# Two-tile cluster transposes, a block-diagonal coarse product, and other engines for the last two pairs of a fused language-model layer

## What is computed

```python
fine_emb = fine_embed_w[location_ids]                                   # 64 columns
cluster_logits = loc_to_cluster_w.T[location_ids] + loc_to_cluster_b    # 64 clusters
cluster_dist = softmax(cluster_logits, axis=-1)
coarse_emb = einsum('bsc,ch->bsh', cluster_dist, coarse_embed_w)        # 64 columns
h = concatenate([fine_emb, coarse_emb], axis=-1)
...
# per expert e, with gate weight g of each token for each expert
y += g * (silu(x @ w_gate[e].T) * (x @ w_up[e].T)) @ w_down[e].T
```

## Time and profile before

| | |
|---|---|
| time, median of 3 runs | 710.78 us (710.51 to 711.16) |
| profiled execution | 710.27 us |
| its span, first to last instruction | 708.1 us |
| TensorE's granted clock over it | 1.000 |
| busy: PE, DVE, ACT, POOL | 693.4 (98%), 472.1 (67%), 389.5 (55%), 465.6 (66%) us |
| mean DMA rate over the span | 113 GB/s |

### The profile page before, as it was taken

The page is one execution under the profiler, slowest core; times in us unless marked ns, Lnnn a source line. Parts: engine busy times, 40 slices in busy tenths (PEclk is TensorE's granted clock), DMA queues, the critical chain, the costliest instruction groups (busy, mean ns, idle before and its releaser), DMA issues.

```text
span 708.1 us, 10029 instructions
## 1 busy us (share of the span) xinstructions
PE 693.4 (98%) x3130; PEld 521.2 (74%) x3130; DVE 472.1 (67%) x976; ACT 389.5 (55%) x719; POOL 465.6 (66%) x359
## 2 busy tenths in 40 slices
PE   8789999999999999999999999999999999999998
PEld 7766776777777777777777777777777777777775
DVE  5687666775686765966578756876669555774443
ACT  3555466548456566557565484565665555534333
POOL 5036776766768567777577666685676666676664
PEclk9999999999999999999999999999999999999999
DMA  5504332333233333253233332343333433344431
GB/s 201 235 0 126 124 104 101 116 115 106 89 121 124 105 120 104 84 148 96 100 110 116 112 114 90 119 124 100 120 104 91 132 99 106 112 122 120 137 120 59
DMA packets 48869, 80.17 MB, mean 113 GB/s; under 512 B 9520, under 2 KB 13744, under 8 KB 48816
## 3 DMA queue, kind: packets, MB, share of 16 engines
q1 hardware_dynamic: 47792, 77.44, 34.6%
q0 software_dynamic: 1024, 2.10, 1.3%
HBM read 76.35 MB, written 3.15 MB: 112 GB/s over the span
## 4 chain that ended last, share of the span: by engine, by line
PE 89%; DVE 4%; issue 2%; ACT 1%; POOL 1%; DVEq 0%; ACTq 0%; POOLq 0%
PE bank_y L487 16%; PE bank_g L504 8%; PE bank_u L504 8%; PE bank_u L506 8%; PE bank_u L505 8%; PE bank_g L506 8%; PE bank_g L505 8%; PE bank_y L484 4%; PE bank_y L482 4%; PE bank_y L481 4%; PE bank_f L406 1%; PE bank_f L428 1%; PE bank_f L465 1%; PE bank_f L422 1%; PE bank_f L439 1%
## 5 line engine op out<-in xcount | busy, mean ns | idle before, releaser
L1145 POOL TENSOR_TENSOR hid<-hid,gate_rows 128x512 f32<-128x512 f32 x256 | 370.9, 1460 | 195.2 <-DVE hid L961 193.6
L961 DVE TENSOR_TENSOR hid<-hid,bank_u 128x512 f32<-128x512 f32 x258 | 175.3, 683 | 172.7 <-PE bank_u L506 93.4
L680 ACT ACTIVATE hid<-bank_g 128x512 f32<-128x512 f32 x264 | 156.8, 597 | 209.6 <-PE bank_g L506 201.4
L487 PE MATMUL bank_y<-hid,w_down 128*128 128x512 f32 x280 | 142.7, 592 | 0.1
L504 PE MATMUL bank_g<-x_hi,gate_hi 128*128 128x512 f32 x264 | 141.4, 536 | 0.8 <-ACT hid L680 0.8
L974 DVE TENSOR_TENSOR hid_lo<-hid,hid_hi 128x512 fp32r<-128x512 f32 x124 | 115.1, 928 | 1.0 <-ACT hid_hi L686 0.5
L504 PE MATMUL bank_u<-x_hi,up_hi 128*128 128x512 f32 x264 | 104.9, 397 | 0.3 <-DVE hid L961 0.3
L506 PE MATMUL bank_u<-x_lo,up_hi 128*128 128x512 f32 x264 | 104.8, 397 | 0.0
L505 PE MATMUL bank_u<-x_hi,up_lo 128*128 128x512 f32 x264 | 104.1, 395 | 0.0
L506 PE MATMUL bank_g<-x_lo,gate_hi 128*128 128x512 f32 x264 | 103.9, 394 | 0.0
L505 PE MATMUL bank_g<-x_hi,gate_lo 128*128 128x512 f32 x264 | 103.8, 393 | 0.0
(11 more groups left out here) (223 smaller groups left out, 845.8 us busy)
## 6 DMA issues: line engine op xcount, KB each, us to landing
gate_rows<-gates_dram SPq DMA_DIRECT2D x512, 128.0 KB, 2.9
w_down<-down_t_dram SPq DMA_DIRECT2D x3, 704.0 KB, 14.5
out_dram<-later SPq DMA_DIRECT2D x7, 256.0 KB, 3.1
hid<-gate_t_dram SPq DMA_DIRECT2D x2, 704.0 KB, 6.6
gates_dram<-gates_t SPq DMA_DIRECT2D x8, 128.0 KB, 2.3
gate_rows<-up_t_dram SPq DMA_DIRECT2D x1, 704.0 KB, 5.9
later<-up_t_dram SPq DMA_DIRECT2D x1, 704.0 KB, 10.2
raw<-gate_t_dram SPq DMA_DIRECT2D x1, 704.0 KB, 11.2
```

What stands on the lines that cost most here:

```text
L487: pe.matmul(y, w_down[:, p, :], hid[:, slot(par, p), :], start=(p == 0), stop=(p == PAIRS - 1)).then_inc(sem("down_done"), 1)
L680: act.activation(hid[:, slot(par, p), :], bank_g[(p + par) % 2][:, :], ACT.Silu).then_inc(sem("silu"), 1)
L961: dve.tensor_tensor(hid[:, s, :], hid[:, s, :], bank_u[(p + par) % 2][:, :], ALU.mult)\
L1145: pool.tensor_tensor(hid[:, s, :], hid[:, s, :], gate_rows[:, row, :], ALU.mult)\
```

## The change

Three things change.

1. The transposes take two tiles at once: 128 tokens x (2 x 64) clusters become a 128x128 block, so there are two where there were four, and the result fills 128 partitions x 256 columns. ACT's copy has that shape too.
2. The coarse weight is laid out block-diagonally in a 128x128 tile, zeroed by a DVE memset and filled by two DMAs, which SP issues after a wait for the memset. Two matmuls with 128 rows and 128 columns take the place of four with 64 rows and 64 columns; the output lies as it did.
3. In the last sequence pair 31 is no longer split, and pair 32's gate weights are multiplied on by DVE in place of POOL. DVE does it at the end of its list, after its own product of pair 32, and TensorE's last `down` waits for that.

```diff
-        coarse_sb = sb("coarse_sb", [CLUSTERS, HALF])
+        coarse_sb = sb("coarse_sb", [P, 2 * HALF])
...
-        lge_t = z[0:CLUSTERS, :, :].rearrange("p t d -> p (t d)")
+        lge_t = z[:, 0:2, :].rearrange("p t d -> p (t d)")
...
         def is_split(b, p):
-            return p % 2 == 1 and (b > 0 or p > 8)
+            return p % 2 == 1 and (b > 0 or p > 8) and not (b == BATCHES - 1 and p == PAIRS - 2)
...
-            sp.dma_start(coarse_sb[:, :], coarse_w).then_inc(sem("coarse_w"), 16)
+            sp.wait_ge(sem("coarse_zero"), 1)
+            for k in range(2):
+                sp.dma_start(coarse_sb[k * CLUSTERS:(k + 1) * CLUSTERS, k * HALF:(k + 1) * HALF], coarse_w)\
+                  .then_inc(sem("coarse_w"), 16)
...
                 alone(pe, "pe_passed")
-                for t in range(TILES):
-                    last = pe.transpose(f1[0:CLUSTERS, t * P:t * P + P], lg[:, t, :], ident[:, :])
+                for k in range(TILES // 2):
+                    two = lg[:, 2 * k:2 * k + 2, :].rearrange("p t e -> p (t e)")
+                    last = pe.transpose(f1[:, k * P:k * P + P], two, ident[:, :])
                 last.then_inc(sem("pe_exp_t"), 1)
...
                 pe.wait_ge(sem("exp_t"), b + 1)
-                for t in range(TILES):
-                    last = pe.matmul(f0[:, t * HALF:t * HALF + HALF], lge_t[:, t * P:t * P + P], coarse_sb[:, :],
-                                     start=(t == 0), stop=(t == TILES - 1), skip_group_check=True)
+                for k in range(TILES // 2):
+                    last = pe.matmul(f0[:, k * P:k * P + P], lge_t[:, k * P:k * P + P], coarse_sb[:, :],
+                                     start=(k == 0), stop=(k == TILES // 2 - 1), skip_group_check=True)
                 last.then_inc(sem("pe_coarse"), 1)
...
-                pe.wait_ge(sem("gated"), q + 1)
+                if b == BATCHES - 1 and p == PAIRS - 1:
+                    pe.wait_ge(sem("gated_last"), 1)
+                else:
+                    pe.wait_ge(sem("gated"), q + 1)
...
-            pe.wait_ge(sem("coarse_w"), 16)
+            pe.wait_ge(sem("coarse_w"), 32)
...
-                act.activation(lge_t, banks[1][0:CLUSTERS, :], ACT.Copy).then_inc(sem("exp_t"), 1)
+                act.activation(lge_t, banks[1][:, 0:TILES // 2 * P], ACT.Copy).then_inc(sem("exp_t"), 1)
...
             dve.memset(ones[:, :], 1.0).then_inc(sem("ones"), 1)
+            dve.memset(coarse_sb[:, :], 0.0).then_inc(sem("coarse_zero"), 1)
...
                     dve_lo(dve, last, 1, p)
+            row, s = (PAIRS - 2) % GATE_RING, slot(1, PAIRS - 1)
+            dve.wait_ge(sem(f"gate_rows{row}"), 32 * (ROUTED_PAIRS // GATE_RING) * BATCHES)
+            dve.wait_ge(sem("up_used"), PAIRS * BATCHES)
+            dve.tensor_tensor(hid[:, s, :], hid[:, s, :], gate_rows[:, row, :], ALU.mult).then_inc(sem("gated_last"), 1)
             dve.wait_ge(sem("stored"), 16 * BATCHES)
...
         def pool_sequence(pool, b, par, late, early):
-            for p in range(PAIRS):
+            for p in range(PAIRS - 1 if b == BATCHES - 1 else PAIRS):
```

## The result

The changed kernel takes 703.57 us, the median of three executions (703.29 to 703.65), against 710.97 us for the kernel before beside it (710.51 to 711.55): a ratio of 0.9895, 95% interval 0.9875 to 0.9914. A fourth execution was disturbed (3937 us) and is in none of these numbers. Run again, the changed kernel gave the same ratio, 0.9895 (0.9878 to 0.9911). The forecast was 704.0, with a range from 703.2 to 705.6.

What follows compares the result with a forecast made beforehand. TensorE was taken to bound the loop, a chain through all engines the prologue, a short tail the end. 4.71 + 1.10 + 0.92 - 0.02 = 6.71 us off 710.27 gives 703.6; plus 0.5 for the median, forecast 704.0, range 703.2 to 705.6.

Steps and rivals of the forecast that it cites:

- Coarse product: Loop, sequences 2 to 7: four passes at 0.111 us replace eight at 0.154; 0.785 us saved each, 4.71 in six.
- the dear bound: Coarse product if each pass keeps its present price: 4 x 0.154 = 0.62 us, so 0.61 saved a sequence.
- Transposes: Cluster weights in the loop: two for four at 0.11 us each, 0.22 saved in five sequences, 1.10; nothing in sequence 2.
- Loop as a whole: Savings of the coarse product and the cluster transposes in the loop together: 5.81 us.
- Prologue: Sequence 0's embedding: transposes 0.22, ScalarE's copy 0.21, coarse product 0.49 us saved, 0.92 in all, transposes starting at 11.73.
- rival that the gain is hidden: Prologue's gain lost to a weight chunk's landing or a later wait; only the loop's 5.81 remains, 705.0 us; chance 0.12.
- the third chunk: Prologue weight chunk arriving by DMA, landing near 19.6 us, copied at 20.8; a 0.92 move still finds it, margin 0.3.
- Start: Second weight block's 0.17 us memset on VectorE and extra small DMA on SP, covered by waits; cost 0.
- End: Last sequence: plain pair 31 takes 0.86 us for 0.84, pair 32's multiplication on VectorE is ready in time; +0.02 us.
- ScalarE late: Loop: SiLU comes too late for the shorter transposes, turning the 1.10 us saved into waits; 705.2 us; chance 0.06.
- The clock rival: Prologue: TensorE's granted clock falls to 1.2 GHz, slowing 6.7 us or more of work; 710 to 714 us; chance 0.04.
- The total: Sum of loop, prologue and end savings: 6.71 us off the profiled 710.27, giving 703.6 us.

Runs made afterwards that it cites:

- third experiment: Changed kernel with the coarse product's rows halved: two matmuls of 64 rows and 128 columns, second tile of each pair left out; 706.08 us, ratio 0.9933.
- first experiment: Changed kernel with the block-diagonal weight read as four products of 128 rows and 64 columns instead of two of 128 columns; 707.10 us, ratio 0.9944.

## Why the prediction was right, point by point

- **Coarse product: right in size.** 0.785 us a sequence forecast, 0.79 measured (1.23 to 0.44, the gate product's normal 0.23 left out of both). The suspect was right, the 64-row tile; the division by passes was not, as the 64-row product with four passes shows: 0.84 where the dear bound had 0.62. The bound was no bound, and the value taken held because the new tile has 128 rows. The prediction's remark that the trace speaks against a load's time going by columns alone is wrong too: loads take 187 ns with 64 rows and 190 with 128, and it is when a load starts that differs.
- **Transposes: right.** 0.11 each at either width, and sequence 2's turned into waiting (0.44 for 0.23).
- **Loop as a whole:** 5.81 forecast, 6.0 measured. The 0.2 more is 5 x 0.02 in the sequences and 0.09 that a neighbouring group of transposes in sequence 0 gave (0.44 and 0.26 on the chain where it had 0.47 and 0.32).
- **Prologue: the term that was mis-sized,** 0.92 forecast, 0.40 at the first gate product. The profile with 38 warm-ups, whose transposes start at 11.73 as before, gives the steps:

```profile
12.18 0.38 ACT L679 ACTIVATE z<-bank_y 128x256 f32<-128x256 f32 x1 [0.55 <-PE bank_y L463]
...
12.62 0.71 PE L469 MATMUL bank_y<-coarse_sb,z 128*128 128x128 f32 x4
...
13.37 0.42 DVE L942 TENSOR_TENSOR emb<-bank_y,soft 128x256 f32<-128x256 f32 x1 [0.85 <-PE bank_y L469]
```

  Transposes 0.18 (for 0.22), copy 0.21 (for 0.21), product 0.38 (for 0.49, whose low end was 0.41), 0.77 in all, and 0.76 of it came through to the gate product there (86.61 for 87.37). The product fell short because the prediction took the loop's prices, with their surcharge for the 64-row tile, into the prologue. There the weights are what ScalarE's copy has just written, so no load can go ahead, and the rows cost the product itself nothing. Four passes take 0.71 us with 64 rows (third experiment) as with 128, and eight take 1.10 with 128 rows (first experiment) as with 64:

```profile
12.72 0.71 PE L469 MATMUL bank_y<-coarse_sb,z 64*128 64x128 f32 x4
```

```profile
12.75 1.10 PE L470 MATMUL bank_y<-coarse_sb,z 128*128 128x64 f32 x8
```

  The rest of the shortfall in the changed kernel's first profile is the start, 0.31 later, behind slow warm-ups. The prediction took 11.73 as fixed; the trace of one execution can't show that it isn't. The rival that the gain is hidden fell: the third chunk held up nothing, and what the rows gained came through to the gate product but for 0.1.
- **Start: right,** no cost. The memset took 0.17 us under VectorE's wait, which went from 3.42 to 3.34, and the weight chunks were issued at 9.8 as before.
- **End: right,** 0.02 of loss forecast, 0.01 measured, and as two effects that cancel. But the prediction gave the whole end as one sum; taken apart, one half of it is worth 0.15 us and the other costs as much.
- **ScalarE late: fell.** No wait for a SiLU in the loop but sequence 0's.
- **The clock rival:** its price was off and its argument wrong. "No idle stretch gets longer" was argued from waits that shrink, but TensorE's idle stretch ahead of L374 went from 1.85 to 2.04 us, because the work before it became shorter by more than the rows came earlier. The grant does fall there in some executions, of both kernels, at a price of about 1 us; the 6.7 us and more of slow work on the path that the rival needed never came, since the fall is over after about 3 us. It isn't seen more often in the changed kernel, with 1 of 7 executions.
- **The total** of 6.71 met the 6.70 of the profiled executions by luck in two places: 0.5 too much in the prologue, against 0.2 too little in the loop and 0.3 outside the span. The forecast of 704.0 also had 0.5 us on top, by which the median of the kernel before stood above its profile; the changed kernel's median is the profiled execution itself, which is about the 0.43 us by which the forecast missed.

## What to carry to other kernels

Read what a small matmul adds to the path from the chain of waits together with the instruction behind it, and look at the weight loads' own timeline: a load that starts with its matmul and not ahead of it is on the path. A change of tile rows in a stream of full tiles cost about 0.2 us going in and as much coming out here, so zeros that fill a tile up to 128 rows can be cheaper than a product that fits. Split a change with two halves into two terms, since halves that cancel can hide a gain (0.16 us of the end here, seen in the profile and not in the times), and read the start of a prologue from more than one execution before tenths of a microsecond are counted in it.

## What the runs showed of the hardware that was not expected

- A weight load of 64 rows behind one of 128, or the reverse, didn't start ahead of its matmul: 0.33 to 0.40 us for the two switches around a group, whether it had eight passes or four. A tile of 128 rows and 64 columns had no such price, and neither had the product in the prologue, whose load has to wait for its weights anyway.
- The first 20 transposes of the same code took 3.86 to 4.53 us, which held up the work behind them in one of 14 profiles, by 0.3 us; in the others the gathered embeddings set the start. The Trainium skill (TensorE: Matmul & The Clock Gate, section What's actually happening) says that the number of slow matmuls at a start varies from run to run for one kernel; the traces agree in so far as the burst's time varies; how many of its matmuls were slow was not counted.
- With 0.73 us of idling ahead of a burst of transposes the clock fell in none of 12 executions, with 1.85 to 2.05 in 35 of 68. The warm-up burst before the shorter stretch was longer by as much, so the two aren't told apart.
